# Softmax attention: the reciprocal of the softmax sums moved from VectorE to ScalarE and GpSimd

## The reference

```python
x = x + jnp.tanh(g_xattn[0]) * _L0_xattn_ref(_layernorm(x, axis=-1), ctx_2048, ...)

# inside _L0_xattn_ref, with 8 heads of 8 channels over 256 positions
q = _apply_rotary(q_emb, split_heads(_proj(x, Wq, bq)))
k = _apply_rotary(k_emb, split_heads(_proj(c, Wk, bk)))
v = split_heads(_proj(c, Wv, bv))
scores = jnp.einsum('bhtc,bhsc->bhts', q, k) / math.sqrt(K_CH)
p_attn = jax.nn.softmax(scores, axis=-1)
out = jnp.einsum('bhts,bhsc->bhtc', p_attn, v)
```

## Time and profile before

| | us |
|---|---|
| median of three runs | 2600.49 (2599.89 to 2602.58) |
| span of the profiled execution | 2704.4 |
| PE busy | 2250.3 |
| DVE busy | 1841.5 |
| ACT busy | 1152.8 |
| POOL busy | 1105.8 |

### The profile page before, as it was taken

One profiled execution on the slowest core, in us unless ns is written; L12 is line 12 of the kernel. 1 busy time (PEld: TensorE's weight loads), 2 busy tenths in 40 slices (PEclk: granted clock), 3 DMA queues, 4 the chain that ended last, 5 costly groups with the idle time before them and its releaser, 6 DMA issues. The chain is left out here.

```text
span 2704.4 us, 60407 instructions
## 1 busy us (share of the span) xinstructions
PE 2250.3 (83%) x20880; PEld 1699.7 (63%) x20880; DVE 1841.5 (68%) x3965; ACT 1152.8 (43%) x2509; POOL 1105.8 (41%) x1111
## 2 busy tenths in 40 slices
PE   6889989786878579994799899899888699998890
PEld 4555555443766357773677777787766577886670
DVE  4888888762547567775878878878876365444654
ACT  2777667554434223332344444444333354332230
POOL 2455555554144400001445445455577301325526
PEclk9898899765889689997999999999999799999995
DMA  5555455433358431211332332332334462445644
GB/s 115 125 134 141 121 137 131 113 114 100 104 178 277 133 130 52 64 31 51 82 83 62 81 85 59 81 87 57 85 100 135 134 206 90 142 148 167 200 153 144
DMA packets 249859, 313.10 MB, mean 116 GB/s; under 512 B 45152, under 2 KB 202848, under 8 KB 249056
## 3 DMA queue, kind: packets, MB, share of 16 engines
q1 hardware_dynamic: 188592, 219.11, 28.9%
q0 software_dynamic: 26624, 58.79, 7.9%
q10 hardware_dynamic: 34352, 31.34, 3.4%
HBM read 122.40 MB, written 102.24 MB: 83 GB/s over the span
## 5 line engine op out<-in xcount | busy, mean ns | idle before, releaser
L2119 POOL TENSOR_TENSOR ca_qk<-ca_qk,ca_q_swap 128x512 f32<-128x512 f32 x160 | 249.9, 1562 | 371.2 <-DVE ca_q_swap L2297 369.6
L735 DVE TENSOR_REDUCE soft_top<-soft_pa 128x2 fp32r<-128x512 f32 x512 | 328.4, 683 | 99.6 <-PE soft_pa L816 81.8
L630 ACT ACTIVATE soft_prob<-soft_pb 128x512 f32<-128x512 f32 x512 | 286.0, 594 | 191.8 <-PE soft_pb L809 171.9
L809 PE MATMUL soft_pb<-soft_rep 32*128 32x256 f32 x1024 | 213.4, 368 | 62.1 <-DVE soft_top L735 39.6
L809 PEld LDWEIGHTS soft_pb<-soft_rep 32*128 32x128 f32 x1024 | 140.1, 218 | 181.8 <-issue 85.8
L1440 PE MATMUL moe_pgu<-moe_w_hi,moe_xt_hi 128*128 x472 | 198.1, 420 | 39.8 <-DVE moe_xt_lo L1357 24.9
L816 PE MATMUL soft_pa<-soft_rep 31*128 31x256 f32 x1024 | 223.0, 375 | 6.0 <-DVE soft_top L735 3.5
L1459 PE MATMUL moe_py<-moe_w_d,moe_at 128*128 x788 | 219.1, 394 | 1.7 <-issue 0.8
L1363 DVE TENSOR_TENSOR moe_act_f<-moe_silu,moe_pgu 128x256 f32<-128x256 f32 (+1 forms) x236 | 88.5, 375 | 165.4 <-ACT moe_silu L1258 111.2
L2389 PE MATMUL ca_py<-ca_w_hi,ca_ot_hi 128*128 128x256 f32 x512 | 154.4, 302 | 33.1 <-DVE ca_ot_lo L2318 32.8
L1258 ACT ACTIVATE moe_silu<-moe_pgu 128x256 f32<-128x256 f32 (+1 forms) x236 | 82.1, 348 | 230.0 <-PE moe_pgu L1440 149.8
(11 more groups left out here) (377 smaller groups left out, 6384.7 us busy)
## 6 DMA issues: line engine op xcount, KB each, us to landing
ca_q_swap<-ca_q_f SPq DMA_DIRECT2D x640, 64.0 KB
moe_xs<-moe_rows SPq DMA_DIRECT2D x236, 128.0 KB
soft_rep<-soft_parts SPq DMA_DIRECT2D x378, 64.0 KB
moe_rows<-soft_blank SPq DMA_DIRECT2D x27, 768.0 KB
moe_ys_rows<-moe_ys ACTq DMA_DIRECT2D x134, 128.0 KB
moe_ys<-moe_ys ACTq DMA_DIRECT2D x102, 128.0 KB
moe_xd<-scratch SPq DMA_DIRECT2D x64, 128.0 KB
ca_vs<-ca_v SPq DMA_DIRECT2D x32, 256.0 KB
```

The source lines that it names most:

```text
L630: act.activation(prob[:, k % 4, h, :], p_b[:, 2 * T * h:2 * T * (h + 1)], ACT.Exp).then_inc(prob_ready, 1)
L735: dve.tensor_reduce(heads[:, j, :, g], p_a[:, 2 * T * h:2 * T * (h + 1)].rearrange("p (c s) -> p c s", c=HALF), AX, ALU.max).then_inc(a_do ...
L809: mm = pe.matmul(p_b[:, out], rep[of, i % 4, g, at:at + PART], rep[of, i % 4, g, 0:T], start=True, stop=True)
L2119: pool.tensor_tensor(qk[:, u % 2, m, :], qk[:, u % 2, m, :], q_swap[:, p % 2, :], ALU.add).then_inc(qk_ready, 1)
```

## The change

DVE's reciprocal goes away. ACT takes the logarithm of the sums and then exp(-log), a first estimate of the reciprocal, behind exp 7 and ahead of everything else at the end of its step. POOL refines it by one Newton step, on the product rather than on the reciprocal: `off = sums * r`, `packed = packed * r`, `off = 2 - off`, `on = packed * off`. Before the loop ACT loads the table set that holds both functions.

```diff
+        log_sum, off = sb("log_sum", [PART, T]), sb("off", [PART, T])
+        log_ready, refined = sem("log"), sem("refined")
...
# POOL
                         pool.wait_ge(rsum_ready, t + 1)
                         past(pool, wo_ready, t - 1)
-                        pool.tensor_tensor(on[:, t % 2, :], packed[:, t % 2, :], rsum[:], ALU.mult).then_inc(on_ready, 1)
+                        pool.tensor_tensor(off[:], sums[:, t % 2, :], rsum[:], ALU.mult).then_inc(refined, 1)
+                        pool.tensor_tensor(packed[:, t % 2, :], packed[:, t % 2, :], rsum[:], ALU.mult).then_inc(refined, 1)
+                        pool.wait_ge(refined, 3 * t + 2)
+                        pool.tensor_scalar(off[:], off[:], -1.0, 2.0, ALU.mult, ALU.add).then_inc(refined, 1)
+                        pool.wait_ge(refined, 3 * t + 3)
+                        pool.tensor_tensor(on[:, t % 2, :], packed[:, t % 2, :], off[:], ALU.mult).then_inc(on_ready, 1)
# ACT, before the loop
                 act.activation(gate[:], cols[:, 6:7], ACT.Tanh).then_inc(gate_ready, 1)
+                act.preload_act_table_set("natural_log_exp_and_others")
# ACT, in the loop
                     exp(i, 7)
+                    t = i - 1
+                    if live(t):
+                        act.wait_ge(pack_in[t % 2], PACK * (t // 2 + 1))
+                        act.activation(log_sum[:], sums[:, t % 2, :], ACT.Ln).then_inc(log_ready, 1)
+                        past(act, on_ready, t)
+                        act.wait_ge(log_ready, t + 1)
+                        act.activation(rsum[:], log_sum[:], ACT.Exp, scale=-1.0).then_inc(rsum_ready, 1)
# DVE, at the end of the step
-                    t = i - 1
-                    if live(t):
-                        dve.wait_ge(pack_in[t % 2], PACK * (t // 2 + 1))
-                        past(dve, on_ready, t)
-                        dve.reciprocal(rsum[:], sums[:, t % 2, :]).then_inc(rsum_ready, 1)
```

## The result

The changed kernel took 2615.47 us (median of 6 runs, 2604.14 to 2622.87), the kernel before 2603.32 in its six; ratio 1.0046, interval 1.0027 to 1.0065. Twelve more runs beside 35 of the kernel before gave 1.0023 (0.9999 to 1.0048). The forecast was 7.5 us slower, 2608; the two measurements say 12 and 6, and the second one by itself just reaches down to no change.

The account below looks back on a forecast made before the run. PE and DVE were both near full, with ACT's short list ending last at quiet seams. Terms -12 + 7 + 2.5 + 2 + 5.3 = +4.8 us, plus 3 for the clock, gave 2608 us, range 2584 to 2627.

Parts of the forecast that it names:

- DVE's part: Seams between tiles: DVE loses 32 reciprocals of 1744 ns, of which 12 us were to be gained.
- the late seams: Seven seams where DVE is late behind routing work or at the loop's thinner end; 10.4 us to be gained.
- ACT's work: End of ACT's step: logarithm and exponential ahead of y add 0.8 us a tile; 7 plus 2.5 us lost.
- the quiet one: Sample seam at full clock without extra routing work; PE waits for y, so ACT's added 0.8 us should delay it.
- PE gets all of it: In nine seams waiting for y, ACT's 0.8 us passes wholly to PE: about 7 us.
- The wait for the sums: Moves from DVE to ACT, ahead of parts, y and the next exponentials; 2 us lost, from 0 to 5.
- POOL: Three more operations on POOL, 2.1 us a tile, from 1.7 to 2.5.
- Hidden in mid-loop: POOL's added 2.1 us a tile disappears in its spare time before the packing, 2.7 us per wait.
- The end: Last tiles of the softmax stage, bare of cover: barrier 5.3 us later, bounds 3 and 8.
- Table loads: One at the preload, one at the next stage's gate, 1.28 us each; both hidden in ACT's idle time.
- The clock: PE's granted clock in the seams: 5.8 us won back in late ones, 8.7 lost in quiet ones, +3 us.
- the second rival: Whole kernel, a wash: seam gains and losses cancel with the clock, or the tail halves; 2596 to 2605, chance 0.20.

Follow-up runs that it names:

- the second trace of before: The kernel before, unedited, profiled once more because its first trace was unusually long; one run, 2600.91 us, span 2599.1.
- The two activations alone: Two spare 128x256 activations ahead of scale, turned, parts and y: 0.9972 in the kernel before, 0.9924 in the kernel without the division.
- the wait alone: ACT waits for the sums ahead of y and does nothing there: 0.9986 in the kernel before, 0.9933 in the kernel without the division.
- the mended version: The change with logarithm and exponential moved behind y; ratio 0.9944 to the kernel before.
- the version with the early wait: The change with logarithm and exponential behind y, but the wait for the sums left ahead of y; ratio 1.0002, 2606.6 us.
- the two mended versions: The change with logarithm and exponential behind y, 0.9944; and the same with tiles 28 to 31 divided as before, 0.9949, 2590.8 us.

## Why the prediction was right, and where it was not

*DVE's part* was forecast at 12 us and 5.8 of clock. Leaving the reciprocal out gave 17 us in the loop; the change with ACT's work behind y has a loop 20 us shorter than before. Right. The forecast rested on the late seams: the second trace of before has a wait of 3.8 us for the maxima at 524, the change one of 1.9 at 523, less by about one reciprocal.

*ACT's work* was forecast at 0.8 us a tile and is 0.83; the projection waits for y in 21 and 24 seams, 0.8 us and more in 15 and 16 of them, and 0.95 us more in the quiet one. But the step from there to time failed: "PE gets all of it", 9.5 us. The two activations alone raised PE's waits for y by 8 us in two kernels and the time in neither. In those two kernels a microsecond of idle PE at that seam was not a microsecond of the loop.

*The wait for the sums* was the term that was mis-sized: forecast 2 us, where ACT stood 16.1 and 15.3 us and the wait alone, put back into the mended version, cost 15. I had scaled it from DVE's four waits of 4.1 us, with ACT arriving up to 1 us earlier than DVE. It arrives 1.8 us earlier: by the median over some 30 tiles DVE asks for the sums 6.1 us after the last of their transfers is issued (both traces of before), ACT in the change 4.2 and 4.3 us after, and ACT with the logarithm behind y again 6.1 and 6.1. So 1.8 of the 3 us and more that the prediction saw to spare are gone. In the change the transfer takes between 2.1 and 6.9 us from issue, 3.3 in the middle:

```profile
DMA to landing us min/median/max: 2.1/3.3/6.9
```

so a reader that asks after 4.2 us instead of 6.1 meets the slow ones. What makes a transfer slow was not tested; at the seam of 378 the transfer of the peaks was late too, in a stretch of heavy traffic.

That the same wait cost nothing measurable in two kernels with a short list on POOL stays open. In both it stood without the two functions. It may be wait and work together that cost. The change without the Newton step has both ahead of y: it takes 17 us more than the kernel without the division, 5 to 7 of them at the end, while the activations alone and the wait alone cost 0 and 2. In the version with the early wait both stand ahead of exp 0. These are differences between groups, near the limit of what can be told apart. The Newton step may add to it: some 5 us in the loop where the wait is early, and nothing where all stands behind y (530.1 us with it, 533.5 in the kernel without the division). One reading is a ring: ACT's wait delays parts, POOL's split behind it, the Newton step and the next packing. The spare time before the packing, 66 us down to 28, speaks for it; that the waits stayed at 16.8 us without the Newton step speaks against it. No run here has the early wait and the Newton step without logarithm and exponential ahead of exp 0, so these readings are not parted.

*POOL* was forecast at 2.1 us a tile: from the start of `off` to that of `on` it is 632.61 - 630.63 = 1.98. The tensor_scalar is 400 ns, not 650. "Hidden in mid-loop" holds for ACT's waits, which stayed without the Newton step, but perhaps not for the 5 us or so that came back in the loop.

*The end* was forecast at 5.3 us from the last exponential on. There it is 28.9 us in both traces of the change, 22.3 and 23.6 in those of before, so 5.3 to 6.6 longer. From the last copy of the peaks it is 3.2 to 6.6 (49.0 and 51.1 against 44.5 and 45.8), and undoing it gave 5.5 in time, inside the interval. Right, by the mechanism described: the packing of the last tile starts 10.5 us after the last exponential (639.16 - 628.65) instead of 5.1 and 6.5, so 4.1 to 5.4 later where 4.1 was forecast. POOL's rows of the change, with this packing behind the sends, then its start in the second trace of before:

```profile
630.63 0.72 POOL L609 TENSOR_TENSOR soft_off<-soft_sums,soft_rsum 128x256 f32<-128x256 f32 x1 [3.17 <-ACT soft_rsum L689]
...
632.61 0.72 POOL L614 TENSOR_TENSOR soft_on<-soft_packed,soft_off 128x256 f32<-128x256 f32 x1
...
639.16 0.65 POOL L594 DMA_DIRECT2D soft_packed<-soft_o_raw  x1
```

```profile
633.49 0.64 POOL L592 DMA_DIRECT2D soft_packed<-soft_o_raw  x1
```

*Table loads*: ten instead of eight, none in the loop. At the next stage ACT's first xt_hi comes 2.81 us after its first instruction (660.35 - 657.54), before 2.85 (668.51 - 665.66) and, in the second trace, 2.61: the extra load of 1.28 us costs 0.2 us at most. The drain that the Trainium skill adds (ScalarE: Activation LUTs, What ACT_TABLE_LOAD costs) does not show here either: the activation starts at 658.83, 0.01 us after the load. ACT had been idle ahead of that load, but at another, from 717.27, it was not: the instruction before ended 0.02 us earlier, and the next one starts at 718.57, 0.02 us after the load.

*The clock* was forecast to take 3 us. Over the same 530 us of the loop the granted clock reads 0.88 and 0.85 in the two traces of before, 0.89 and 0.88 in those of the change, and 0.89 and 0.92 in the two mended versions; here the second of before, then the change (stretch and length, busy us and instructions of PE, its weight loads, DVE, ACT and POOL, then the clock, DMA share, GB/s):

```profile
56.00:586.00 530.00, 476.10 (x4372) 286.25 (x4372) 442.18 (x894) 363.12 (x787) 279.91 (x404) 0.85 0.52 132
```

```profile
56.00:586.00 530.00, 454.17 (x4356) 272.67 (x4360) 400.95 (x863) 380.75 (x836) 327.67 (x483) 0.89 0.52 131
```

PE is busy 22 us less in the change, in part because its matmuls are shorter at the upper level. But two traces of one kernel differ by 0.03 here, nearly as much as the kernels do, and over whole runs the middle clock is 0.916 to 0.917 for the change and 0.918 for the kernel before. So no loss by the clock is seen, and neither the size nor the sign of that term is shown.

The sum left out most of the wait (2 for 15) and counted 9.5 us for y, which no run shows as a price of its own. These two errors point in opposite directions. That the total came out near, between the 6 and the 12 us measured, is luck in the loop; only DVE's part and the end were right by their own mechanism. A slip on which nothing hangs: the untouched part of the kernel is 2004 of 2704 us, 74%, not the 69% that the second rival names.

## What to carry to other kernels

When work moves to an engine with time to spare, ask what stands behind it in that engine's order, and move the wait that comes with it to where nothing is urgent behind it: here one place in the list, behind y instead of ahead of it, is the difference between 0.2 to 0.5% slower and 0.6% faster. The same early wait cost 15 us in one version and nothing that shows in another, so its price has to be measured in the kernel in which it will stand. Compare the time at which the reader will ask with a transfer's slowest landing, not with its median. Bare ends of a pipeline deserve a sum of their own.

## What the runs showed of the hardware

- Ln and Exp on 128x256 take 416 ns each in the change, near a copy (386), with no table load between them in a set that has both.
- GpSimd's tensor_scalar on 128x256 takes 400 ns in the change, its tensor_tensor 727.
- The kernel before spread over 2590 to 2620 us in 28 runs on one chip. Its two traces differ by 15 us in this one stage; the granted clock over the same stretch was 0.88 in the longer and 0.85 in the shorter.
- Eight microseconds more of PE waiting for y did not show in the time, twice (ratios 0.9972 against 1, and 0.9924 against 0.9925).
- The transfers of the sums, four of 32 KB a tile issued by GpSimd, took 2.1 to 6.9 us from issue to landing in the change, 3.3 in the middle.
